# Two of sixteen state products moved from GpSimd to VectorE, the z projection moved into the next turn, and an output projection in two parts, in a two-layer AdaLN megakernel

## The reference

```python
xz = hidden_states @ in_proj_w.T
x, z = jnp.split(xz, 2, axis=-1)             # 512 channels each
x = silu(causal_conv4(x) + conv_b)
dt, k, q = jnp.split(x @ x_proj_w.T, [64, 80], axis=-1)   # k, q: 16 states
dt = dt @ dt_head_w.T
def step(state, inp):                        # state: 512 x 16
    dtv = sigmoid(dt_t + dt_head_b)
    dtv = dtv / (1.0 + dtv * sum(k_t * k_t))
    state = state * (1.0 - dtv[..., None] * kk[:, None, :]) + (x_t * dtv)[..., None] * k_t[:, None, :]
    y_t = einsum('bdn,bn->bd', state, q_t)
    return (state, y_t)
y = (ys + D * x) * silu(z)
out = y @ out_proj_w.T
```

## Time and profile before

| | us |
|---|---|
| median of 3 runs (lowest, highest) | 1822.53 (1820.58, 1823.0) |
| profiled execution, its time | 1821.96 |
| its span | 1820.2 |
| PE busy (share of the span) | 1657.9 (91%) |
| DVE busy | 1469.9 (81%) |
| POOL busy | 1369.6 (75%) |
| ACT busy | 1314.7 (72%) |

### The profile page before, as it was taken

One profiled execution on the slowest core, in us unless ns is written; L12 is line 12 of the kernel. 1 busy time (PEld: TensorE's weight loads), 2 busy tenths in 40 slices (PEclk: granted clock), 3 DMA queues, 4 the chain that ended last, 5 costly groups with the idle time before them and its releaser, 6 DMA issues.

```text
span 1820.2 us, 33709 instructions
## 1 busy us (share of the span) xinstructions
PE 1657.9 (91%) x12156; PEld 1424.5 (78%) x12156; DVE 1469.9 (81%) x3084; ACT 1314.7 (72%) x2689; POOL 1369.6 (75%) x644
## 2 busy tenths in 40 slices
PE   6678999999999999999999999997777999999998
PEld 5557788887878888787878878786665888899997
DVE  3548889898988988898898889889897678766663
ACT  3568878888887888878788888876643855666664
POOL 0009899999989999999999999999998343444443
PEclk9899999999999999999999999999997999999999
DMA  5011111212111221221122122112112444455552
GB/s 198 1 56 44 71 66 71 73 68 83 68 68 65 76 83 54 82 76 60 65 76 83 53 83 76 59 61 97 65 70 93 116 128 99 122 139 140 137 136 29
DMA packets 69462, 149.78 MB, mean 82 GB/s; under 512 B 5936, under 2 KB 43312, under 8 KB 68912
## 3 DMA queue, kind: packets, MB, share of 16 engines
q1 hardware_dynamic: 57008, 130.84, 20.7%
q0 software_dynamic: 12288, 16.79, 5.2%
HBM read 121.91 MB, written 17.30 MB: 76 GB/s over the span
## 4 chain that ended last, share of the span: by engine, by line
PE 63%; DVE 14%; ACT 12%; issue 6%; POOL 4%; DMA 0%; DVEq 0%; ACTq 0%; POOLq 0%
PE po L1834 10%; PE ph L1834 9%; DVE room L1179 8%; PE pD L1130 8%; PE pY L1147 7%; PE pA L731 6%; POOL room L1188 3%; PE pB L926 3%; PE pB L936 3%; PE pB L1226 3%; ACT room L1160 2%; PE pA L722 2%; PE pB L957 2%; PE pB L942 2%; PE pA L652 1%
## 5 line engine op out<-in xcount | busy, mean ns | idle before, releaser
L1198 POOL TENSOR_TENSOR room<-room 128x1024 f32<-128x1024 f32 x256 | 608.2, 2376 | 159.4 <-DVE room L1113 139.0
L1179 DVE TENSOR_TENSOR_SCAN room<-pD,last,room 128x256 f32<-128x256 f32 x1024 | 688.7, 731 | 38.3 <-PE pD L1130 26.0
L1188 POOL TENSOR_TENSOR room<-room 128x1024 f32<-128x1024 f32 x256 | 607.8, 2375 | 46.4 <-PE pY L1147 46.2
L1160 ACT ACTIVATE room<-room,kkT 128x512 f32<-128x512 f32 x512 | 359.8, 715 | 57.4 <-PE pD L1130 55.9
L1130 PE MATMUL pD<-fixed,room 128*128 128x128 f32 x2048 | 318.1, 279 | 70.1 <-DVE room L1179 60.5
L1147 PE MATMUL pY<-fixed,room 128*128 128x128 f32 x2048 | 315.6, 277 | 15.1 <-POOL room L1188 15.0
L1130 PEld LDWEIGHTS pD<-fixed,room 128*128 128x128 f32 x2048 | 239.1, 143 | 103.2 <-issue 53.4
L1147 PEld LDWEIGHTS pY<-fixed,room 128*128 128x128 f32 x2048 | 246.2, 144 | 66.8 <-POOL room L1188 30.8
L343 POOL DMA_INDIRECT xg<-xn_rows,W x64 | 67.5, 1055 | 196.5 <-DVE W L337 180.9
L1793 ACT ACTIVATE h<-ph 128x512 f32<-128x512 f32 x128 | 76.6, 598 | 137.9 <-PE ph L1834 101.4
L1834 PE MATMUL po<-w_up,h_up 128*128 128x256 f32 x512 | 149.5, 292 | 3.2 <-DVE h_rest L1701 2.6
(11 more groups left out here) (313 smaller groups left out, 3400.0 us busy)
## 6 DMA issues: line engine op xcount, KB each, us to landing
room<-kq_rows SPq DMA_DIRECT2D x128, 512.0 KB, 3.6
w_in<-w_d SPq DMA_DIRECT2D x32, 1024.0 KB
room<-ndS SPq DMA_DIRECT2D x16, 512.0 KB, 3.2
xt<-x_in SPq DMA_DIRECT2D x16, 256.0 KB, 2.9
y_out<-xo SPq DMA_DIRECT2D x16, 256.0 KB, 2.1
xn_rows<-xnC SPq DMA_DIRECT2D x16, 256.0 KB, 2.2
W<-weights SPq DMA_DIRECT2D x1, 1808.0 KB, 8.8
W<-weights SPq DMA_DIRECT2D x1, 1697.5 KB, 16.4
```

The costliest lines, as they stand in the source:

```text
L1160: act.activation(decT[:, m % 2, t, :], turn2(ndT, it, NT * DI, t * DI, DI), ACT.Copy, bias=1.0, scale=turn2(kkT, it, NT * DS, t * DS + m, ...
L1179: dve.tensor_tensor_scan(run, pD[h][:, k2 * TB:(k2 + 1) * TB], run, last[:, bass.ds(later(it) * (DS * DT) + m * DT + k, 1)], ALU.mult, ALU ...
L1188: pool.tensor_tensor(sq[:, m % 2], st[:, m % 4], kqb[:, m % SLOTS, 1, :].unsqueeze(1).broadcast_to([P, DT, TB]), ALU.mult).then_inc(sem("r ...
L1198: pool.tensor_tensor(st[:, m % 4], turn2(u, it, DT * TB).rearrange("p (k t) -> p k t", k=DT), kqb[:, m % SLOTS, 0, :].unsqueeze(1).broadca ...
```

## The change

1. `BY_DVE = (3, 5)`: the `rd` of states 3 and 5 leaves POOL. PE makes the two q rows itself, by two matmuls with a broadcast column of the identity as weights (`rows_q`, step 31) into bank `pB[0]`, and DVE multiplies (`rd_dve`, steps 33 and 39). `pB[0]` holds `x_scan`'s operand until then, so `rows_q` waits for `x_scan`.
2. z's projection and its Silu move from steps 46 to 52 of their own turn to steps 67 to 70, that is 3 to 6 of the next turn. They use bank `pA[1]` in place of `pB[1]`, and so wait for `og`. `dt0` no longer waits for `sz`.
3. `out` becomes `out0` (step 25) and `out1` (step 28); `x_scan` moves from step 28 to 30, where the code issues it behind `x_ffn`.
4. `stat_a` moves from step 0 to step 46 of the turn before; SP issues the load of x it needs ahead of one `spread`.

```diff
@@ AT (values that change)
-    inz0=50, sz0=46, inz1=51, sz1=52, out=25, x_scan=28
+    inz0=67, sz0=68, inz1=69, sz1=70, out0=25, out1=28, x_scan=30, stat_next=46, rows_q=31, rd_dve0=33, rd_dve1=39
...
             for t in range(NT):
                 if n == AT[f"inz{t}"]:
                     if t == 0:
-                        pe.wait_ge(sem("xs"), it * 2 + 1)
+                        pe.wait_ge(sem("og"), upto(it + 1) + 1)
                     else:
                         pe.wait_ge(sem("sz"), it * 2 + 1)
                     for c in range(DC):
-                        i = pe.matmul(pB[1][:, :], hB[:, c, t * P:(t + 1) * P], inproj[:, c, DI:2 * DI],
+                        i = pe.matmul(pA[1][:, :], hB[:, c, t * P:(t + 1) * P], inproj[:, c, DI:2 * DI],
                                       start=(c == 0), stop=(c == DC - 1))
...
-                    if t == 0:
-                        pe.wait_ge(sem("sz"), it * 2 + 2)
-                    else:
+                    if t == 1:
                         pe.wait_ge(sem("kk"), it * 3 + 2)
...
-                    act.activation(turn2(szT, it, NT * DI, t * DI, DI), pB[1][:, :], ACT.Silu).then_inc(sem("sz"), 1)
+                    act.activation(turn2(szT, it, NT * DI, t * DI, DI), pA[1][:, :], ACT.Silu).then_inc(sem("sz"), 1)
...
+            if n == AT["rows_q"]:
+                if back is not None:
+                    pe.wait_ge(sem("x_scan"), back + 1)
+                else:
+                    pe.wait_ge(sem("hT_b"), (it + 2) * DC)
+                for j, m in enumerate(BY_DVE):
+                    row = ident_s[P - 2 * DS:, P - DS + m:P - DS + m + 1].broadcast_to([2 * DS, P])
+                    i = pe.matmul(pB[0][:, j * TB:(j + 1) * TB], row, dkq[P - 2 * DS:, :], start=True, stop=True)
+                i.then_inc(sem("rows_q"), 1)
...
+            for j, m in enumerate(BY_DVE):
+                if n == AT[f"rd_dve{j}"]:
+                    dve.wait_ge(sem("rows_q"), it + 1)
+                    dve.wait_ge(sem("scanned"), it * DT * DS + DT * m + DT)
+                    dve.wait_ge(sem("summed"), it * 2 * DS + 2 * m - 2)
+                    dve.tensor_tensor(sq[:, m % 2], st[:, m % 4],
+                                      pB[0][:, j * TB:(j + 1) * TB].unsqueeze(1).broadcast_to([P, DT, TB]), ALU.mult)\
+                        .then_inc(sem("read_dve"), 1)
...
-            if 0 <= m < DS:
+            if 0 <= m < DS and m not in BY_DVE:
                 pool.wait_ge(sem("scanned"), it * DT * DS + DT * m + DT)
```

More of the change, by code:

```diff
@@ L50 @@
 XBUF = 4
+BY_DVE = (3, 5)
 LRQ = 32
@@ L60 @@
 AT = dict(
-    stat_a=0, ln_a=2, rows_a=4, turn_a=6, mod_a=7, low=8, v=17, lr=14, v_s=17, z=21, abs=21, exl=23, gk=27, G0=27,
+    stat_a=0, stat_next=46, ln_a=2, rows_a=4, turn_a=6, mod_a=7, low=8, v=17, lr=14, v_s=17, z=21, abs=21, exl=23, gk=27, G0=27,
     G1=28, eG0=25, eG1=27, ends=28, q0=31, k0=33, queries0=36, keys0=36, sc0=39, kgt0=38,
@@ L66 @@
     rows_c=33, turn_c=35, mod_c=34, halo=38, inx0=38, xcp0=38, inx1=43, xcp1=44, tail=45, conv0=43, conv1=47,
-    xs0=45, xs1=46, inz0=50, sz0=46, dkq_mm=50, dkq=52, inz1=51, sz1=52, kturn=53, kk=53, dt0=53, dt1=55, sig0=54,
-    sig1=56, den=57, nd=60, ut=61, u=69, yz0=19, yz1=19, yt0=21, yT0=20, yt1=22, yT1=22, out=25, x_scan=28, ln_d=40,
+    xs0=45, xs1=46, inz0=67, sz0=68, dkq_mm=50, dkq=52, inz1=69, sz1=70, kturn=53, kk=53, dt0=53, dt1=55, sig0=54,
+    sig1=56, den=57, nd=60, ut=61, u=69, yz0=19, yz1=19, yt0=21, yT0=20, yt1=22, yT1=22, out0=25, out1=28, x_scan=30, ln_d=40,
     rows_d=42, turn_d=74, mod_d=75, score=79, scores=81, dec=11, sum=22, open0=21, open1=24, dec_t=6, saved=21,
-    scan=13, rd=23, inp=14)
+    scan=13, rd=23, inp=14, rows_q=31, rd_dve0=33, rd_dve1=39)
 PER_BLOCK = dict(
@@ L81 @@
     k_turn=1, kk=3, dt_mm=2, sig=2, den_ln=1, den=1, ndt=1, nd_in=16, ut_mm=2, u=2,
-    inp=DS, dec_t=2 * DS, dec_mm=2 * DS, scanned=DT * DS, saved=DS, read_out=DS, summed=2 * DS, opened=2,
-    yz=2, y_turn=2, yT=2, glast=1, out_mm=1, score_mm=1, scores=1)
+    inp=DS, dec_t=2 * DS, dec_mm=2 * DS, scanned=DT * DS, saved=DS, read_out=DS - len(BY_DVE), rows_q=1, read_dve=len(BY_DVE), summed=2 * DS, opened=2,
+    yz=2, y_turn=2, yT=2, glast=1, out_mm=2, score_mm=1, scores=1)
 PER_BLOCK.update({f"ln{n}_{what}": 1 for n in "abcd" for what in ("rows",)})
@@ L639, in attn_pe @@
                 after(pe, "og", it)
+                if it > 2:
+                    pe.wait_ge(sem("sz"), it * 2 - 2)
                 if it == 1:
@@ L848, in scored @@
                     .then_inc(sem("att"), 1)
-            if n == AT["stat_a"]:
+            if (it, n) == (1, AT["stat_a"]) or (it < NB and n == AT["stat_next"]):
+                new = it if n == AT["stat_a"] else it + 1
                 settled(dve)
-                dve.wait_ge(sem("x_in"), (it + 1) * 16)
-                ln_stats(dve, it, "a", lambda t: x_at(it, t))
+                dve.wait_ge(sem("x_in"), (new + 1) * 16)
+                ln_stats(dve, new, "a", lambda t: x_at(new, t))
             if n == AT["gk"]:
@@ L922, in front_pe @@
                         pe.wait_ge(sem("x_scan"), back + 1)
+                    if m == 1:
+                        pe.wait_ge(sem("read_dve"), it * len(BY_DVE))
                     for k in range(2):
@@ L1003, in front_act @@
                     if m == 0:
-                        after(act, "out_mm", it - 1)
+                        after(act, "out_mm", 2 * it - 2)
                     act.wait_ge(sem("in_x"), it * 2 + m + 1)
@@ L1114, in front_dve, with wait_read, scan_pe @@
                                       flat(xs[:, 2 * kp:2 * kp + 2, :]), ALU.mult).then_inc(sem("u"), 1)
+        def wait_read(eng, it, m):
+            if m < 0:
+                it, m = it - 1, m + DS
+            if m in BY_DVE:
+                eng.wait_ge(sem("read_dve"), it * len(BY_DVE) + BY_DVE.index(m) + 1)
+            else:
+                by_pool = [n for n in range(DS) if n not in BY_DVE]
+                eng.wait_ge(sem("read_out"), it * len(by_pool) + by_pool.index(m) + 1)
         def nth(n, name, every):
             return (n - AT[name]) // every if (n - AT[name]) % every == 0 else -1
-        def scan_pe(pe, it, n):
+        def scan_pe(pe, it, n, back):
             half = nth(n, "dec", 2)
@@ L1144, in scan_pe @@
                 if t == 0:
-                    pe.wait_ge(sem("read_out"), it * DS + m + 1)
+                    wait_read(pe, it, m)
                 for k in range(DT):
@@ L1220, in back_pe @@
                     i.then_inc(sem("y_turn"), 1)
[L1221 to L1224, removed]
+            for t in range(NT):
+                if n == AT[f"out{t}"]:
+                    pe.wait_ge(sem("yT"), it * 2 + 2)
+                    opf = oproj_g[:, :, :, :].rearrange("p b k n -> p (b k n)")
                     for k in range(DT):
@@ L1526, in spread @@
             def spread(it, n):
-                sp.wait_ge(sem("read_out"), it * DS + n + 1 - SLOTS + 1)
+                for m in (n - SLOTS, n - SLOTS + 1):
+                    if m in BY_DVE:
+                        sp.wait_ge(sem("inp"), it * DS + m + 1)
+                    else:
+                        wait_read(sp, it, m)
                 pair = kq_d[bass.ds(it % 2, 1)].rearrange("o r t -> o (r t)")[:, 2 * n * TB:2 * (n + 2) * TB]
@@ L1551, in turn_sp @@
                              xo[:, :, :]).then_inc(sem("x_out"), 16)
+            if a is not None and i >= 1 and not (isinstance(i, int) and i + 3 > NB):
+                sp.wait_ge(sem("x_in"), (i + 3) * 16)
+                load(i + 3)
             if s is not None:
@@ L1557, in turn_sp @@
                              xnC[:, :, :]).then_inc(sem("rows_out"), 16)
-            if a is not None and i >= 1 and not (isinstance(i, int) and i + 3 > NB):
-                sp.wait_ge(sem("x_in"), (i + 3) * 16)
-                load(i + 3)
             if s is not None:
```

9 lines of the change are left out of this document (5 added, 4 removed).

## The result

The changed kernel takes 1974.94 us (median of 4 runs, 1972.27 to 1977.04) against 1821.55 us before (4 runs, 1820.2 to 1823.0): a ratio of 1.084, 95% interval 1.082 to 1.086. It is slower by 153 us; the forecast was 1905, slower by 83, with a range up to 1945. The direction was right, and the time lies outside the range.

A forecast was written before the change was run, and what follows sets the result against it. No engine is full; a 79.0 us turn is a loop through several queues. 13 full turns x 6.2 = 81, turn 1 +4, turns 15 and 16 -2: 1821.96 + 83 = 1905 us, range 1860 to 1945.

The forecast's parts named there:

- Loads on the loop: ACT, full turn: of nine added table loads, three ahead of hB and one in the gate delay the loop, 1.30 us each.
- The fourth, in the gate: Load between the gate's Exp and Ln on ACT: Ln ends 6.3 us late, and `gk` starts 5.4 late.
- the walk: Following one turn's loop step by step, how many us later each starts: hB 5.4, `kk` 8.7, `dt1` 6.3.
- the one at the decays: ACT's table load at `decays`: costs nothing, because ACT used to wait there for `gk` and `G0`.
- The Trainium skill's price of a switch: 2.66 us a switch, drain included: four loads on the loop would add 5.5 us more a turn, time near 1977.
- Ln and Exp from one load: Rival, layer norms and gate: two more loads a turn, not nine; a turn 3.6 us longer, 1870 us; chance 0.05.
- The wait of `rows_q`: PE, behind `wout`: stands still 1.8 us for `x_scan`, a new wait, with the query projection queued behind it.
- DVE to `kk`: DVE, scans to `kk`: 3.4 us more work less 2.25 us of given-up waits, from 7.65 late to 8.7 late.
- PE's clock falls in its new pauses: Part of the rival "worse": slower PE clock or dearer loads, above 1945 us, chance 0.06; the forecast charged nothing for it.
- The upper bound: Top of the range: a full turn of 88 us gives 1945 us.
- the tail: Turns 15 and 16: POOL's 4.65 us less in each, against late `dec_t` and DVE's 2.3 us, together -2 us.
- The gain: Between `xs` and `dkq`: z's two projections gone, 3.44 us, but `dt1` waits for `kk`, using up 2.4 us of slack.

The follow-up runs named there:

- the clock held up: The changed kernel, waits unchanged, with matmuls that nobody reads put into PE's two pauses (ahead of the transposes of xnB and of the q rows): 1925.21 us, ratio 1.058.
- the loads alone: The kernel before, nothing moved, asking for Silu's table set ahead of ln_b, so a full turn holds the changed kernel's 14 loads: 1911.41 us, ratio 1.050.
- both repairs: The changed kernel with the Ln-and-Exp set asked for behind z's second Silu (7 loads) and x_scan ahead of x_ffn: 1894.92 us, ratio 1.041.
- With the pause filled: The kernel before with the nine added loads, plus four matmuls that nobody reads in the pause ahead of the transposes of xnB: 1900.86 us, ratio 1.045.

## Why the prediction came out as it did

- **Loads on the loop.** Right for the three ahead of hB: each took its 1.30 us, and hB was 5.6 us late (forecast 5.4). The fourth, in the gate, hardly shows: with the clock held up Ln is 6.5 us late, `gk` 5.5, as the walk had it (6.3 and 5.4). That the loads alone cost 5.2 us a turn, four times 1.30, is chance: there the gate's load reaches the loop only together with the one at the decays, which was called hidden, by a `dec_t` behind both. In the changed kernel with the clock held up the `dec` behind `wout` stands still for about 0.2 us only, so there the load at the decays is hidden.
- **The Trainium skill's price of a switch.** The prediction quoted the Trainium skill, page "ScalarE: Activation LUTs", section "What ACT_TABLE_LOAD costs", by which the time would be near 1977. The measured 1974.94 is close to that, and for another reason: the trace of after shows Ln 1.30 us behind the load's start (871.00 and 872.30), no drain, and with the same 14 loads the kernel takes 1925 us once PE is kept busy. A sum that comes out right isn't yet the mechanism.
- **Ln and Exp from one load** (a rival). Wrong here: x45 each at L566 and L569.
- **The wait of `rows_q`.** Right in place and nearly in size: 1.39 us against 1.8.
- **DVE to `kk`.** The products were sized right. The step took off 2.25 us of waits that DVE would give up; with PE slow it still waits 0.78 us before the scans at 888.75 and 1.2 us behind them, 2.0 in all (0.6 with the clock held up), because the slow projection had made PE late too. So `kk` is 3.1 us later than the scans were, where the step had 1.05.
- **The step that failed:** "PE's clock falls in its new pauses. [...] 75.9 of 85.2 lies between, and I charge nothing." It compared the busy share of whole turns. What counted was the pauses themselves, which the prediction had worked out: PE with nothing to do while ACT does Ln, load and Exp, and 1.8 us at `rows_q`. Charged by the rows above, `low`, `dec` and `sum` cost about 0.43 us more each, `rows_q` 0.3 and the query projection 1.36 (3.35 against 1.99): some 3.0 us a turn, 39 us in 13 turns, against 49.7 measured by filling the pauses. 1905 + 39 would have been 1944.
- **The upper bound.** 88 us a turn, with the sum's own terms, give 1821.96 + 13 x 9 + 2 = 1941 and not 1945. The measured time lies above both.
- **Open.** 1925 with the clock held up is still 20 us above 1905: 1.1 us in each full turn, 1.9 in turn 1, and some 5 in the tail, which was to gain 2 and lost 3. In a full turn it isn't one term: hB is 5.6 us late, `wout` 6.4, the scans 8.0, `kk` 9.4 and `dt1` 7.3, each step within 0.4 of its forecast. Turn 1 and the tail I didn't take apart.
- **The gain.** z out of the way between `xs` and `dkq` was worth what its new place cost, 2.1 us each by the walk: the move with its loads (1912.55) equals the loads alone (1911.41).

## What to carry to other kernels

When a function moves on ACT, list the table loads in the whole queue before and after, and ask for the shared set right behind the moved function; here that alone is worth 47 to 55 us. When a change makes PE wait where it didn't, count, as a bound, the matmuls behind the wait at half clock as well as the wait, place by place and not by a mean busy share. And where an engine waits anyway, let it first do what another engine waits for: one step in a table, `x_scan` ahead of `x_ffn`, gave back 45 us of 153.

## What the runs showed that I had not expected

A short wait can bring PE's clock down or not. In the changed kernel some 1.4 us of wait at `rows_q` were followed by a slow query projection (3.17 to 3.78 us) in all 13 full turns. Without z's move the wait is longer, 1.66 us or more, and the projection is slow in four of 13 turns only, which last 84.14 to 84.49 us in place of 82.46. Two turns of that kernel:

```profile
832.51 1.12 PE L1162 MATMUL pB<-dkq,fixed 32*128 32x256 f32 x4 [1.67 <-DVE xo L1288]
833.57 2.97 PE L732 MATMUL pA<-hA,W 128*128 128x256 f32 x8
...
916.68 1.12 PE L1162 MATMUL pB<-dkq,fixed 32*128 32x256 f32 x4 [1.67 <-DVE xo L1288]
917.73 1.99 PE L732 MATMUL pA<-hA,W 128*128 128x256 f32 x8
```

The Trainium skill, page "TensorE: Matmul & The Clock Gate", section "Part 1: The HAM clock gate (the "warmup" mystery)", has two levels, 1.2 GHz behind idle time and 2.4 GHz behind sustained work; the rows agree with the levels (a granted clock of 0.50 and 1.00, and 1.03 and 0.60 us for a `sum`, with some fixed time in each). They don't show which wait of such a length will cost something.

Three kernels with different work settle at the same turn: 85.32 to 85.34 us with the loads alone, with z's move alone, and in the last turns with both repairs. With the pause filled the first of them goes to 84.24. What holds the three at one length was not tested.
